# A graph network in one launch: where ScalarE copies rows for the first scatter, and where VectorE forms the layer's messages

## The reference, cut to what matters

```python
x = layernorm(x + L0(x))   # (1+eps)*x + segment_sum(relu(x[src] + edge_attr_48), dst)
x = layernorm(x + L1(x))   # relu(h @ W.T + b), h = cj * segment_sum(x[src] * ci[src], dst), or x where no edge ends
x = layernorm(x + L2(x))   # relu(agg @ W.T + b), agg = segment_sum(norm * x[dst], src)
x = layernorm(x + L3(x))   # gate MLP of edge_attr_40 * x[dst] * cutoff, summed by src
```

## Time and profile before

| | us |
|---|---|
| median of 3 runs | 2671.04 |
| lowest and highest run | 2667.68 and 2671.83 |
| span of the profiled execution | 3047.5 |
| update, second and third turn with their copies (789 to 868) | 79 |
| second dense pass (868 to 1235) | 367 |
| gate (1247 to 1476) | 229 |

### The profile page before, as it was taken

One profiled execution on the slowest core, in us unless ns is written; L12 is line 12 of the kernel. 1 busy time (PEld: TensorE's weight loads), 2 busy tenths in 40 slices (PEclk: granted clock), 3 DMA queues, 4 the chain that ended last, 5 costly groups with the idle time before them and its releaser, 6 DMA issues.

```text
span 3047.5 us, 12805 instructions
## 1 busy us (share of the span) xinstructions
PE 633.7 (21%) x2848; PEld 506.5 (17%) x2848; DVE 1926.7 (63%) x2735; ACT 632.0 (21%) x1121; POOL 1858.8 (61%) x1768
## 2 busy tenths in 40 slices
PE   1111600000028875554422100001430000000000
PEld 0000300000028765443422100001330000000000
DVE  2001799999717766754623825997349999948872
ACT  1001800222113332211211101322112223221110
POOL 4774002777766664556175757777556676574776
PEclk8555955555555555666555555555555555555555
DMA  3110086787014433322860193443122223110000
GB/s 118 22 22 13 1 323 231 257 322 269 16 34 142 142 125 103 86 53 55 49 46 13 18 71 114 130 137 119 50 59 72 87 69 103 58 41 9 17 16 15
DMA packets 158467, 276.20 MB, mean 91 GB/s; under 512 B 88601, under 2 KB 113507, under 8 KB 158259
## 3 DMA queue, kind: packets, MB, share of 16 engines
q1 hardware_dynamic: 96675, 206.39, 24.0%
q0 software_dynamic: 56448, 44.23, 8.7%
q10 hardware_dynamic: 5264, 24.74, 2.2%
HBM read 142.41 MB, written 138.17 MB: 92 GB/s over the span
## 4 chain that ended last, share of the span: by engine, by line
DVE 27%; POOL 22%; issue 16%; another core or an unknown queue 12%; PE 8%; DMA 8%; ACT 7%; SPq 0%; ACTq 0%; DVEq 0%; POOLq 0%
POOL XD L470 7%; POOL out L507 7%; POOL x_table L507 3%; POOL ring L457 3%; PE psT L883 2%; DMA din<-x_table 2%; DMA din<-in_xaux 2%; POOL x_with_degree L507 2%; DVE du L1345 2%; DVE var L1351 2%; DVE psS L1342 2%; DVE do L1362 2%; DMA xa_table<-din 2%; DVE sumb L1270 2%
## 5 line engine op out<-in xcount | busy, mean ns | idle before, releaser
L470 POOL DMA_INDIRECT XD<-xa_table,dstI x196 | 222.1, 1133 | 290.5 <-SPq L360 231.0
L507 POOL DMA_INDIRECT x_table<-sumb,put x196 | 212.6, 1085 | 154.7 <-ACT sumb L619 86.5
L457 POOL DMA_INDIRECT ring<-x_with_degree,srcI x196 | 208.2, 1062 | 146.0 <-DVEq L1426 85.1
L592 ACT ACTIVATE sq<-du 128x1344 f32<-128x1344 f32 x129 | 168.9, 1321 | 536.7 <-DVE du L1345 416.5
L457 POOL DMA_INDIRECT ring<-h_by_src,zs x196 | 214.6, 1095 | 104.0 <-issue 63.5
L457 POOL DMA_INDIRECT ring<-x_table,srcI x196 | 199.5, 1018 | 121.1 <-issue 63.2
L507 POOL DMA_INDIRECT x_with_degree<-sumb,put x196 | 209.6, 1070 | 94.0 <-issue 58.1
L507 POOL DMA_INDIRECT out<-sumb,put x196 | 201.9, 1030 | 94.9 <-issue 60.9
L457 POOL DMA_INDIRECT ring<-edge_records,dstI x196 | 202.2, 1032 | 86.8 <-issue 57.6
L470 POOL DMA_INDIRECT XD<-in_xaux,srcI x196 | 187.7, 958 | 87.9 <-issue 60.3
L1240 DVE TENSOR_SCALAR GX<-GX 128x784 bf16<-128x784 int16 x196 | 74.7, 426 | 253.3 <-remote 204.1
(11 more groups left out here) (322 smaller groups left out, 2907.4 us busy)
## 6 DMA issues: line engine op xcount, KB each, us to landing
din<-in_xaux SPq DMA_DIRECT2D x56, 728.0 KB
xa_table<-din SPq DMA_DIRECT2D x28, 728.0 KB
x_table<-GX SPq DMA_DIRECT2D x28, 686.0 KB
x_with_degree<-GX SPq DMA_DIRECT2D x28, 686.0 KB
din<-x_table SPq DMA_DIRECT2D x28, 686.0 KB
x_table<-do SPq DMA_DIRECT2D x28, 672.0 KB
din<-x_table SPq DMA_DIRECT2D x28, 672.0 KB
out<-do SPq DMA_DIRECT2D x28, 672.0 KB
```

Source lines behind the costliest of these rows:

```text
L457: pool.indirect_dma_start(ring[:, h, t, 0:w], None, table, bass.IndirectOffsetOnAxis(ap=of[:, c * H + t:c * H + t + 1], axis=0), **skip).t ...
L470: pool.indirect_dma_start(XD[:, t, 0:w], None, table, bass.IndirectOffsetOnAxis(ap=of[:, t:t + 1], axis=0)).then_inc(rows[c].sem, rows[c]. ...
L507: pool.indirect_dma_start(table, bass.IndirectOffsetOnAxis(ap=put[:, c * H + t:c * H + t + 1], axis=0), rows_of[:, h, t, :], None, bounds_ ...
L592: nc.scalar.activation(sq[:, h, :, :], u, ACT.Square).then_inc(S["squared"], 1)
```

## The change

ScalarE makes only the copies of chunks 0 and 1 in the update. Chunks 2 to 7 and 11 are copied at the start of pairs 0 to 5 and 8 of the second dense pass (`AT_START`), chunks 8, 9, 10, 12 and 13 at the end of pairs 5 to 9 (`AT_END`). `EARLY` keeps messages 0 and 1, behind pairs 12 and 13. Messages 2 to 12 go to the gate's groups 2, 4, ... 22, and message 13 behind the last group. The degree factor is worked out ahead of the gate into `t0` and copied to `t0P` behind it.

```diff
--- before.py
+++ after.py
@@ -30,8 +30,10 @@
 REC_PAIRS, SRC_PAIRS, LAST_PAIRS = 6, (2, 3, 4, 5), 4
 SORT_P = EP // SORT_C
 GROUPS = -(-CE // 8)
-EARLY = {10: 0, 11: 1, 12: 2, 13: 3}
-MESSAGES = {24 * (c - 3) // 10: c for c in range(4, 14)}
+EARLY = {12: 0, 13: 1}
+MESSAGES = {2 * (c - 1) if c < 13 else GROUPS: c for c in range(2, 14)}
+AT_START = {0: 2, 1: 3, 2: 4, 3: 5, 4: 6, 5: 7, 8: 11}
+AT_END = {5: 8, 6: 9, 7: 10, 8: 12, 9: 13}
 SKIP = float(1 << 20)
 HALF_NODES = NP // 2
 UP, DOWN = 256 - HALF_NODES, 65536 + 256 + HALF_NODES - 1
@@ -671,15 +673,15 @@
                 act.wait_ge(own.sem, own.now())
                 act.sem_inc(S["rows_ready"], 1)
 
-            STAGED = {0: (0, 1), 2: (2,), 4: (3,), 6: (4, 5)}
             for i in range(0, NBLK, 2):
                 norm([(0, su[:, :, :])] + pair[1:] if i + 1 < NBLK else [(0, su[:, :, :])])
-                for c in STAGED.get(i, ()):
-                    to_stage1(c)
+                if i == 0:
+                    to_stage1(0)
+                    to_stage1(1)
 
             def short1(n):
-                if 6 <= n + 5 < CE // H:
-                    to_stage1(n + 5)
+                if n in AT_START:
+                    to_stage1(AT_START[n])
                 ahead = n < DBLK // 2 - 1
                 evacuate(tall=97)
                 if ahead:
@@ -688,6 +690,8 @@
                 if ahead:
                     evacuate((2, 3), 97)
                 roots(pair)
+                if n in AT_END:
+                    to_stage1(AT_END[n])
             evacuate(tall=97)
             given = 0
             for n in range(DBLK // 2):
@@ -700,6 +704,7 @@
                     before(given, given % 2)
 
             function(t1[:, :], ACT.Sin)
+            function(t0[:, :])
             mt, = views("mlp_t")
             mfree = S["mlp_free"]
 
@@ -713,10 +718,8 @@
                     given += 1
                     if given < CE // H:
                         before(given, given % 2)
-            if GROUPS - 1 in MESSAGES:
-                give_back(given, given % 2)
-
-            function(t0[:, :])
+            give_back(given, given % 2)
+
             def update():
                 evacuate()
                 norm(pair[:1])
@@ -1453,6 +1456,9 @@
             ask_act()
             one(V.scalar_tensor_tensor(t1[:, :], t1[:, :], 1.0, t0[:, :], ALU.add, ALU.mult))
             one(V.tensor_tensor(t1[:, :], t1[:, :], nv[:, :], ALU.mult))
+            one(V.tensor_scalar(t0[:, :], cnt[:, :], 1.0, None, ALU.max))
+            ask_act()
+            one(V.reciprocal(t0[:, :], t0[:, :]))
             dve.sem_inc(S["mlp_free"], 3)
             dve.sem_inc(S["z_free"], 2)
             dve.sem_inc(S["mlp_used"], 2)
@@ -1498,12 +1504,11 @@
             V.tensor_copy(GX[:, :, PLACE - D], XD[:, :, D + 2]).then_inc(own.sem, own.add())
             one(V.tensor_copy(GX[:, :, DIS - D], XD[:, :, D + 3]))
             dve.sem_inc(S["rec_ready"], 1)
+            one(V.tensor_copy(t0P, t0[:, :]))
+            messages(MESSAGES[GROUPS] % 2)
             dve.wait_ge(returned.sem, returned.up(2 * NBLK))
             carries(False)
-            one(V.tensor_scalar(t0[:, :], cnt[:, :], 1.0, None, ALU.max))
             dve.sem_inc(S["srt_ready"], 1)
-            ask_act()
-            one(V.reciprocal(t0P, t0[:, :]))
             one(V.tensor_copy(carryP, carry[:, 0:D]))
             mean, inverse, shift = muP, srsP, carryP
```

## The result

The changed kernel takes 2646.77 us (median of 4 runs, 2644.79 to 2647.78) against 2671.36 for the one before: ratio 0.9908, interval 0.9894 to 0.9922, 24.6 us faster. Forecast were 36.1 us, 2635, between 2603 and 2672. In the second of them the changed kernel took 2634.3: 0.9923, interval 0.9910 to 0.9936, about 21 us. One of the 12 runs of the degree factor alone was slow, 3179.4 us, and is left out of its ratio.

The account below looks back on a forecast made before the run. No engine busy throughout: ScalarE's waits for GpSimd's queue delay the dense pass, GpSimd's fills set the gate's end. -63.5 + 7.5 - 17.5 + 38.2 - 1.3 + 0.5 = -36.1 us, 2671 to 2635; range 2603 to 2672.

Parts of the forecast that it names:

- Start of the dense pass: Second dense pass: its first evacuation comes 15.5 us behind the scatter's first DMA instead of 79.1, -63.5 us.
- Doubled copy and single copies: Dense pass: copies 10 and 11 together between pairs 7 and 8 cost 4.5 us, three more single copies 3, together +7.5.
- Pairs 11 and 12: Dense pass: without a message each of these pairs takes 22.6 us instead of 31.34, together -17.5 us.
- Degree factor and message 13: Gate: factor moved ahead of it +0.5 us (bounds -1.4 and +1.4); message 13 alone behind the last group -1.3.
- Two more fills: Gate: ten fills instead of eight follow its first message, 2 x 19.1 = +38.2 us, bounds 6 and 43.
- Hidden extra fills: Gate: standstills are in the runs too, so 38.2 becomes 12: -62 us, 2609 us; chance 0.17.
- Slower through faster GpSimd: Second gather to gate: GpSimd's DMAs take a factor s less in the runs; at 0.88 +16 us, 2687; chance 0.14.
- the cancelling case: Dense start and gate: start gain and fills cancel, s (runs' GpSimd DMA-time factor) near 0.93: 2671 +- 5 us; chance 0.10.
- Fills slowed by VectorE: Gate: VectorE slows fills to 21.5 us, two cost 43, so -31 us, 2640 us; chance 0.12.
- ScalarE's wait for L513: Update: a sign that the forecast is right, ScalarE no longer waits for this line there.
- One wait of some 4 us ahead of copy 11: Dense pass: a sign of being right, a single ScalarE wait of this size before chunk 11's copy.
- line 457 without waits: Gate: a sign of being right, GpSimd's line 457 has no waits for VectorE's L1426 there.

Follow-up runs that it names:

- the second of them: Second of three later sets of runs, each beside the kernel before; the changed kernel, unchanged, took 2634.31 us there, ratio 0.9923.
- the degree factor alone: Kernel before with only the degree factor worked out ahead of the gate and copied to `t0P` behind it: 2655.99 us, ratio 0.9993.
- before, again: The kernel before, unchanged, profiled again because its first profile was 376 us above the median: 2653.41 us, span 2651.5.
- disturbed execution: First profiled execution of the unchanged kernel before, which the prediction's rows come from; 376 us above the median.
- message 2 in its right place: Message 2 in gate group 0, message 3 in group 3: ratio 0.9883 with the changed kernel's copies, 0.9884 with chunks 11 to 13 copied after pairs 8 to 10.
- the copies alone: Kernel before with only ScalarE's copies moved as in the change; messages and degree factor as before: 2643.96 us, ratio 0.996.
- one copy a pair: Changed kernel, but chunks 11, 12 and 13 are copied at the end of pairs 8, 9 and 10: 2630.32 us, ratio 0.9913 to the kernel before.
- messages alone: Kernel before with only the messages moved, 0 and 1 behind pairs 12 and 13, the rest in the gate: 2676.64 us, ratio 1.009.
- later sets: Three later sets holding the experiments, each beside runs of the kernel before, whose medians were 2656.1, 2656.0 and 2656.0 us.

## Why the prediction was half right

Direction, range and the forecast's own range (2620 to 2655) held; the gain was 24.6 and about 21 us, not 36.1. Step by step, counted from the scatter's first DMA, changed kernel against before, again:

- Start of the dense pass: forecast -63.5, measured 77.1 - 11.6 = -65.5.
- **Doubled copy and single copies: forecast +7.5, measured 24.7 us of waits for the stage, 17.53 of them ahead of copy 11; single copies nothing. This is the step that failed.** The prediction had copies a pair of 22.6 us apart and GpSimd 18.6 a chunk, so that GpSimd would be far ahead by chunk 10, and gave 10 us as the worst. The pair's pace came from the disturbed execution. GpSimd's came from the scatter's first 15 DMAs, and for half of them VectorE stood still (the 13.47 us ahead of 812.23). An undisturbed execution alone wouldn't have mended it: the first chunk takes 17.9 us in before, again, and 20.0 in the changed kernel (last section). Undisturbed, a pair takes (872.83 - 811.34) / 3 = 20.5 and a scatter chunk 14 x 278.0 / 195 = 19.96. The first free half is at +21.0 (596.51), nine chunks later chunk 11's is at 575.5 + 21.0 + 179.6 = 776.1; the copy came at 776.95. Two engines in step have no lead, and a copy more must then wait for a chunk.
- Pairs 11 and 12: forecast -17.5. With a message a pair takes 26.9 (881.48 to 908.38), not 31.34, so -12.8. To this point -65.5 + 24.7 - 12.8 = -53.6; between message 2 of before, again (935.48, so +359.9) and message 0 here (+306.0) lie -53.9.
- Degree factor and message 13: forecast +0.5 and -1.3. Ahead of group 2's message +3.0 (32.4 against 29.4 from the message behind pair 13), behind the last fill's start -5.0 (9.7 against 14.7): -2.0 together.
- Two more fills: forecast +38.2; from group 2's message to the last fill 189.1 against 151.8, +37.3.

-53.9 + 3.0 + 37.3 - 5.0 = -18.6, and the update starts 18.7 us earlier. Against -36.1 the doubled copy's 17.2 and the pairs' 4.7 are missing, some 4 come back at the start, in the fills and behind them. The sum is right as bookkeeping of one path through ScalarE and VectorE.

That the range held is in part luck: copy 11's wait alone, 17.53 us, lies beyond the 10 that were given as the worst, and the width that covered it was there for the rivals.

The sum is wrong as a cause. It says that 17 us more would come without the doubled copy; the run that took it away got 3 to 4, within the noise, and with message 2 in its right place no gain can be told (0.9883 against 0.9884). The terms weren't independent: GpSimd is at work without a gap through gather, scatter and fills, and -65.5, +24.7 and -12.8 are ScalarE and VectorE getting to message 0 at the time at which fill 0 is there (872.23 in the run with the copies alone, 877.65 with one copy a pair). What the change gained is 16.5 us of GpSimd's waits (28.1 to 11.6), of which 13.7 are seen at the last fill, and 5.0 behind it. The rest between the two is start and pace: the chain began 1.5 us later (297.1 against 295.6), the gather took 1.6 less, the scatter 4.9 more (278.0 against 273.1 from its first DMA to its last), the fills without their waits 1.9 less. The prediction saw GpSimd set the end of the gate, and that it went from the gather to the scatter with 0.30 us between, but didn't ask whether it had room anywhere from there on.

The rivals. Hidden extra fills: fell (messages alone were slower, and VectorE waits 57.5 us for fills). Slower through faster GpSimd, and the cancelling case: they needed a factor of 0.93 or less, and a chunk took 19.96 against 18.6 in the scatter and 18.8 against 19.1 in the fills, a factor of 0.98. Fills slowed by VectorE: not by as much as was named. Ten took 1129.9 + 0.9 - 942.5 = 188.3 us, 18.8 each, not 21.5, beside a VectorE busy 144.5 of 227 us:

```profile
913.00:1140.00 227.00, 122.92 (x644) 103.70 (x644) 144.51 (x538) 47.34 (x66) 159.69 (x156) 0.67 0.29 63
```

By the rule of the Trainium skill (SBUF — State Buffer, Who interferes with whom) a two-port instruction of VectorE and GpSimd block each other. The rows of the last section do show single DMAs drawn out beside VectorE's instructions. They don't show in which mode those ran, so whether this rule is at work stays open.

Of the marks that the prediction named, ScalarE's wait for L513 did go from the update, VectorE did wait for fills, and no new wait stood behind the gate. The dense pass starts 11.6 us behind the scatter's first DMA, earlier than the 15 to 30 named, and pairs 11 and 12 take 20.5 us, not 22 to 23. "One wait of some 4 us ahead of copy 11" was 17.53, and "line 457 without waits" had one, 9.53 us for message 2, which the prediction had not seen since it counted the fills from that message on.

Open: why the later runs put the gain at 21 and the first at 24.6, though their intervals overlap (both kernels are 12 to 15 us shorter in the later sets); and what would shorten the chain itself, since neither an order of DMAs across the blocks nor another arrangement of VectorE's work beside them was tried.

## What to carry to other kernels

Before adding up what each edit saves, look for an engine whose blocks of work stand end to end, and list its waits: they are the most that taking waits away can give, here 28.1 us plus what stands behind its last instruction. A wait of another engine is worth only what it passes on, so a long one may be all but free (17 us here) and a short one on the chain worth more (moving message 2 by two groups and message 3 by one gave 6 to 8). When the pace of two engines decides whether a copy waits, take both paces from an execution whose span agrees with the runs, and from a stretch in which the other engines work as they will after the change.

## What the runs showed of the hardware

GpSimd's indirect DMAs took 1.43 us a column in the changed kernel's scatter (278.0 / 195), 1.40 in that of before, again (273.1 / 195), and 1.35 in the changed kernel's fills (187.4 / 139). That isn't a pace of their own. Between two DMAs lie 0.30 us; what varies is the DMA. At the start of the scatter VectorE stands still in before, again, and every DMA of the first chunk takes 0.97 to 1.01 us:

```profile
580.77 0.97 POOL L507 DMA_INDIRECT x_with_degree<-sumb,put  x1 [0.30 <-issue]
...
596.90 1.55 DVE L1351 TENSOR_REDUCE var<-sq 128x28 f32<-128x1344 f32 x1 [28.65 <-ACT sq L592]
```

In the changed kernel VectorE isn't held up there. Beside its instructions on two tensors DMAs are longer, beside its reductions they aren't:

```profile
577.00 1.38 POOL L509 DMA_INDIRECT x_with_degree<-sumb,put  x1 [0.30 <-issue]
577.55 1.56 DVE L1338 TENSOR_TENSOR MG<-MG,sub 128x1344 f32<-128x1344 f32 x1
...
583.19 1.60 POOL L509 DMA_INDIRECT x_with_degree<-sumb,put  x1 [0.30 <-issue]
582.38 1.56 DVE L1348 SCALAR_TENSOR_TENSOR sub<-mu,sub 128x1344 f32<-128x1344 f32 x1
...
585.09 0.97 POOL L509 DMA_INDIRECT x_with_degree<-sumb,put  x1 [0.30 <-issue]
585.33 1.55 DVE L1354 TENSOR_REDUCE var<-sq 128x28 f32<-128x1344 f32 x1 [1.39 <-ACT sq L594]
```

So the first chunk takes 17.9 us in the three kernels with the old copies (before, again; messages alone; degree factor alone) and 19.8 to 20.0 in those with the moved ones. Over the changed kernel's 588 DMAs of the three blocks, 202 have nothing of VectorE beside them, or only reductions, reciprocals and reads of its accumulator: they take 0.94 us in gather and fills and 0.97 in the scatter, and one is longer by more than 0.04. Of the other 386, beside other instructions of VectorE, most of them `SCALAR_TENSOR_TENSOR` and `TENSOR_TENSOR`, 184 are, up to 2.3 us. What lies above 0.94 and 0.97 adds up to 81 us of the chain. This is read from one trace, and before, again gives 78 us the same way; no run changed VectorE's instructions alone.

A change of ScalarE's function has a row of its own, 1.28 us. In the changed kernel it ran ahead of a request at 913.78, 917.53 and 1158.72. Where the gate's first Silu waits for TensorE, it came only behind that wait, and the Silu behind it (929.65):

```profile
928.36 1.28 ACT L714 ACT_TABLE_LOAD   x1 [9.16 <-PE psA L978]
```

The one that the prediction feared in the update lies under a variance, and 0.32 us of wait are left:

```profile
1158.72 1.28 ACT L600 ACT_TABLE_LOAD   x1
1160.32 0.32 ACT L600 ACTIVATE std<-var,lneps 128x28 f32<-128x28 f32 x1 [0.32 <-DVE var L1354]
```

The page ScalarE: Activation LUTs of the Trainium skill (What ACT_TABLE_LOAD costs) has 2.66 us with its drain, of which about 1.28 is the load. The rows agree with the load and show nothing of the drain: in the update the root starts 2.94 us behind the squares in both kernels (1157.38 to 1160.32; 1175.99 to 1178.93), with a change of function between them in the changed kernel only.
